# Three Sturm rounds of 7 points instead of two of 20, and 22 pairs of samples beside the Householder steps instead of 21

## The reference

```python
def reference(x, adj, L0_gnn_W1, L0_gnn_W2, L0_gnn_W3, L1_gnn_W1, L1_gnn_b1, L1_gnn_W2, L1_gnn_b2):
    def _slconv(x, adj, S, W):
        support = jnp.einsum('bnf,fh->bnh', x, W)
        return jnp.einsum('nm,bmh->bnh', adj * S, support)
    # layer 0, with S = adj: widths 256 -> 512 -> 1024 -> 256
    h = jnp.maximum(_layernorm(x, axis=-1), 0.0)
    h = jax.nn.relu(_slconv(h, adj, adj, L0_gnn_W1))
    h = jax.nn.relu(_slconv(h, adj, adj, L0_gnn_W2))
    x = x + _slconv(h, adj, adj, L0_gnn_W3)
    # layer 1: widths 256 -> 128 -> 256
    h = jnp.maximum(_layernorm(x, axis=-1), 0.0)
    deg = jnp.sum(adj, axis=0) + jnp.sum(adj, axis=1) - jnp.diagonal(adj)
    d = jnp.where(deg > 0, jax.lax.rsqrt(deg), 0.0)
    _, U = jnp.linalg.eigh(d[:, None] * (jnp.diag(deg) - adj) * d[None, :])
    agg = jnp.einsum('mn,bnd->bmd', U.T, h)
    out = jax.nn.relu(agg @ L1_gnn_W1 + L1_gnn_b1) @ L1_gnn_W2 + L1_gnn_b2
    return x + jnp.einsum('nm,bmd->bnd', U, out)
```

## Time and profile before

| | us |
|---|---|
| median of three runs (lowest, highest) | 2318.28 (2315.64, 2318.72) |
| profiled execution, span | 2315.7 |
| TensorE matmul busy | 2285.6 (99%) |
| TensorE weight load busy | 1884.1 (81%) |
| VectorE busy | 2018.1 (87%) |
| ScalarE busy | 1098.8 (47%) |
| GpSimd busy | 1102.6 (48%) |

### The profile page before, as it was taken

The page is one execution under the profiler, slowest core; times in us unless marked ns, Lnnn a source line. Parts: engine busy times, 40 slices in busy tenths (PEclk is TensorE's granted clock), DMA queues, the critical chain, the costliest instruction groups (busy, mean ns, idle before and its releaser), DMA issues.

```text
span 2315.7 us, 43479 instructions
## 1 busy us (share of the span) xinstructions
PE 2285.6 (99%) x11050; PEld 1884.1 (81%) x11050; DVE 2018.1 (87%) x10266; ACT 1098.8 (47%) x2581; POOL 1102.6 (48%) x1780
## 2 busy tenths in 40 slices
PE   7999999999999999999999999999999999999999
PEld 5777888787787788887777788888888888899998
DVE  8999999999999888878888889799999998467776
ACT  5445555555555444445444444444444444245554
POOL 6345545544444555455544464445555445243332
PEclk9999999999999999999999999999999999999999
DMA  2000000000000000000000000000000001024443
GB/s 103 28 28 28 19 19 28 28 28 25 22 28 28 28 20 18 28 27 28 28 28 28 19 29 28 28 10 28 27 27 27 28 28 37 19 67 130 135 132 108
DMA packets 90018, 89.95 MB, mean 39 GB/s; under 512 B 5376, under 2 KB 89088, under 8 KB 89856
## 3 DMA queue, kind: packets, MB, share of 16 engines
q1 hardware_dynamic: 89856, 88.23, 12.0%
HBM read 54.66 MB, written 33.55 MB: 38 GB/s over the span
## 4 chain that ended last, share of the span: by engine, by line
PE 83%; DVE 12%; ACT 2%; issue 2%; POOL 0%; DMA 0%; SPq 0%; POOLq 0%; DVEq 0%
PE ps L1481 68%; PE ps L1660 10%; PE ps L1393 3%; DVE A L895 2%; DVE A L899 1%; PE ps L1670 1%; ACT squares L624 1%; DVE xrow_sb L904 1%; PE ps L1607 1%; DVE qn L929 1%; ACT root_s L626 1%; DVE prods L932 1%; DVE sc L913 1%; DVE sc L916 1%; DVE qcol L918 1%
## 5 line engine op out<-in xcount | busy, mean ns | idle before, releaser
L1481 PE MATMUL ps<-w,hid2T 128*128 128x256 f32 x2048 | 465.9, 379 | 0.0
L1481 PEld LDWEIGHTS ps<-w,hid2T 128*128 128x128 f32 x2048 | 379.9, 190 | 49.8
L471 POOL COPY Eb<-sc 128x1 f32<-128x1 f32 (+1 forms) x254 | 47.2, 186 | 529.6 <-DVE v L920 297.2
L1481 PE MATMUL ps<-agg2T,w 128*128 128x256 f32 x1024 | 239.0, 379 | 0.0
L1481 PE MATMUL ps<-hid2T,xin 128*128 128x256 f32 x1024 | 235.8, 379 | 0.0
L1481 PE MATMUL ps<-weightT,hid 128*128 128x256 f32 x1024 | 235.6, 379 | 0.0
L1481 PE MATMUL ps<-w,aggT 128*128 128x512 f32 x512 | 231.8, 592 | 0.0
L1481 PEld LDWEIGHTS ps<-weightT,hid 128*128 128x128 f32 x1024 | 190.1, 191 | 35.2 <-issue 13.1
L1092 DVE RECIPROCAL ps<-ahead 128x40 f32<-128x40 f32 (+1 forms) x768 | 218.0, 329 | 0.1
L1481 PEld LDWEIGHTS ps<-agg2T,w 128*128 128x128 f32 x1024 | 190.2, 190 | 25.3
L1481 PEld LDWEIGHTS ps<-hid2T,xin 128*128 128x128 f32 x1024 | 189.3, 190 | 24.6
(11 more groups left out here) (370 smaller groups left out, 5547.7 us busy)
## 6 DMA issues: line engine op xcount, KB each, us to landing
xl<-in_x_dram SPq DMA_DIRECT2D x64, 256.0 KB, 2.9
xr<-in_x_dram SPq DMA_DIRECT2D x64, 256.0 KB, 2.9
x_dram<-xr SPq DMA_DIRECT2D x64, 256.0 KB, 2.3
xin<-x_dram SPq DMA_DIRECT2D x64, 256.0 KB, 2.8
out_dram<-xin SPq DMA_DIRECT2D x64, 256.0 KB, 2.1
w<-in_L_gnn_W_dram SPq DMA_DIRECT2D x1, 2048.0 KB, 10.6
w<-in_L_gnn_W_dram SPq DMA_DIRECT2D x1, 1024.0 KB, 12.2
w<-in_L_gnn_W_dram SPq DMA_DIRECT2D x1, 512.0 KB, 5.9
```

The costliest lines, as they stand in the source:

```text
L471: pool.tensor_copy(Eb[:, bass.ds(k, 1)], sc[:, 4:5])
L1481: ins = pe.matmul(dst, a, b, start=start, stop=stop)
```

## The change

Each of the 256 eigenvalues is now narrowed by three rounds of 7 points in place of two of 20: the interval shrinks by 8 x 8 x 8 = 512 in place of 21 x 21 = 441. W falls from 40 to 14. Three buffers get a size that holds 16 elements, for the first count. In `GROUPS`, pair 11 has 12 steps in place of 13, pairs 16 to 19 have 12 in place of 14, pair 20 has 11 in place of 13, and pair 21 now has 11 steps. So `WITH_STEPS` is 22 and `FIRST_ROUND` 24: the pairs without steps before the transposes of the counts are 22 and 23, the joins stand beside pair 24, and pairs 25 to 29 run alone.

```diff
-KS = 20
-ROUNDS = 2
+KS = 7
+ROUNDS = 3
...
         points = sb("points", [P, NB, KS])
-        negs = sb("negs", [P, ROUNDS_OF * 2 * NB * KS])
-        meet = sb("meet", [P, 3, NB * KS])
-        cnt = sb("cnt", [P, NB * KS])
+        widest = max(C0, NB * KS)
+        negs = sb("negs", [P, ROUNDS_OF * 2 * widest])
+        meet = sb("meet", [P, 3, widest])
+        cnt = sb("cnt", [P, widest])
...
-        GROUPS += [(8, 10, 12, 0.54), (10, 11, 12, 0.54), (11, 12, 13, 0.54), (12, 16, 12, 0.54), (16, 20, 14, 0.54),
-                   (20, 21, 13, 0.54)]
+        GROUPS += [(8, 10, 12, 0.54), (10, 11, 12, 0.54), (11, 12, 12, 0.54), (12, 20, 12, 0.54), (20, 21, 11, 0.54),
+                   (21, 22, 11, 0.54)]
...
-                link(dve.tensor_tensor(below_j[:, :, :], cnt[:, :].rearrange("p (a c) -> p a c", a=NB),
+                link(dve.tensor_tensor(below_j[:, :, :], cnt[:, 0:NB * KS].rearrange("p (a c) -> p a c", a=NB),
```

## The result

The changed kernel takes 2336.5 us (median of four runs, 2335.9 to 2338.1) against 2317.9 for the kernel before: a ratio of 1.008, 95% interval 1.0068 to 1.0092, so 16 to 21 us more, and 18.6 by the medians. The profiled execution has a span of 2336.3 us against 2315.7, 20.6 us more; its own time, 2338.07, is the highest of the four.

The account below looks back on a forecast made before the run. TensorE's matmul list bounds the kernel, so effects are waits: norm 49.9 - 19 - 2.8 = 28.1 us later, TensorE 27.7 later, plus 1.5 for the clock, 29.2 more. Forecast 2347.5 us, range 2336 to 2360.

Parts of the forecast that it names:

- the author's own case: The main forecast for the whole kernel: 2347.5 us, with a range of its own of 2338 to 2357; chance 0.76.
- The steps: TensorE beside pairs 11 to 21: fewer waits and moved steps make its list 8.8 us shorter, within 6 to 11.
- The start of the chain: VectorE's chain behind the transposes of the counts starts 49.9 us later, its 13.35 us wait staying.
- The rounds: VectorE's three rounds take 282 us, within 276 to 290, against 301.1 for two, so 19 us come back.
- The place: One of 128 places in a VectorE round, two reciprocals and two multiply-adds: 0.556 us with 14 elements.
- Company before the norm: Three VectorE instructions just ahead of the norm lose 2.8 us as GpSimd stands too; bounds 0 and 5.
- The standing: TensorE pauses 36 us in pair 30 before P5; ScalarE's square root waits near 41 us for VectorE.
- The clock: TensorE runs slow behind its pause in pair 30, losing 1.5 us, with 0 and 4 as bounds.
- the first: Rival: places no cheaper than with 16 elements, or more VectorE company in three rounds: 2359.5 us, chance 0.10.
- the third and fourth: Rivals on VectorE's place: 0.46 us, giving 2309.5 us, chance 0.04; about 0.48 us, no telling change, chance 0.02.
- a place of 0.76 us: VectorE's place by the skill page's rule of one cycle per element: rounds some 120 us, result about 80 us worse.
- The second: Rival: the square root holds nobody, TensorE stands only at L1619, from 1950.7; 2341 us, chance 0.08.

Follow-up runs that it names:

- e6: The changed kernel with GpSimd's sums made on 2 of 256 columns, so its output is not the reference's: 2319.0 us, ratio 1.0001.
- e5: The changed kernel with the joins of the reflectors from fragment 5 of pair 24 on instead of fragment 10: 2332.9 us, ratio 1.0064.
- e9: The changed kernel with 24 narrow VectorE instructions, forecast at 4.6 us in all, put in front of the first round: 2338.4 us, ratio 1.0088.
- e10: The changed kernel again, unaltered, on the same chip as the run with the delayed chain: 2337.3 us, ratio 1.0082.
- e3: The changed kernel with ScalarE's square root moved behind the evictions of P2 instead of those of agg2: 2338.2 us, ratio 1.0086.
- e4: The changed kernel with the transposes of the counts at fragment 27 of pair 23 instead of behind it: 2325.1 us, ratio 1.0030.
- e1: The kernel before with only the changed rounds, three of 7 points, and the old table of steps beside 21 pairs: 2317.8 us, ratio 0.9998.

## Why the prediction was right, and what was off

The direction and the mechanism were right. The size was not: 29.2 us more were forecast, 18.6 measured by the medians and 20.6 by the spans. The time of 2336.5 lies half a microsecond inside the range of 2336 to 2360, and below the 2338 to 2357 of the author's own case. That it lies inside at all is luck.

- **The mechanism** held step by step: no matmul more or less, TensorE's gain beside the steps, the chain that starts later, the pause in front of the second half of `hid2T,xin` in pair 30, released by ScalarE's eviction of P1, and no second wait at `turn_z`.
- **The steps.** Forecast 8.8 us, measured 9.15; pair 11 62.3 (62.28), pairs 16 to 19 246.0 (245.66), pair 20 61.1 (61.13), pair 21 64.1 (64.17).
- **The start of the chain.** Forecast 49.9 us later, measured 49.5, with the wait of 13.36 us unchanged.
- **The rounds: the term that was mis-sized.** Forecast 282 us, within 276 to 290, so 19 back; measured 272.55, 28.6 back. The place was right: 0.556 us forecast, 0.56 in the rows. What failed is the base it was put on: the 96.6 us of the one count with 16 elements were carried over whole, as a price of the walk. e6 has this count without company at 88.0 us and a round at 85, so some 9 us of company had been put into each of three rounds, where 4 to 7 belong. How much belongs depends on how VectorE's bulk instructions fall among GpSimd's sums: e5, e9 and e10 have 268 to 271 us for the same instructions. The forecast's rate for them, about 1 ns per element, was taken only for the difference between 16 and 14 elements; the whole of the count's bulk instructions, with their meetings in it, should have been taken apart.
- **Company before the norm.** Forecast 2.8 us, measured 1.9: from the eigenvalues to the square root 148.3 us before, 146.4 after. The three instructions did fall to 0.69 us each, but `before_y<-Db,lam` (L1161), just behind the eigenvalues, now met a sum and took 1.65 us instead of 0.69. That standing engines shorten the chain holds only for this stretch: e3 shows the cost of the sums moved, not removed.
- **The standing.** Forecast 36 us, measured 26.0, and ScalarE's wait 31.5 instead of 41: the 9 us of the rounds, and 1.6 by which TensorE came later to P5 than its gain beside the steps, since the pair with the joins was slow.
- **The clock.** Forecast 1.5 us; from P5 to `turn_z` it was 2.0, with a granted clock of 0.50 in the rows. The forecast's size came from a row that does not show the clock: in the stretches of 2 us around the 5.11 us at 12.87 the granted clock reads 1.00, and what slowed that row stays open. (The page's slices, digits of 9, say 0.9 or more.) The Trainium skill ("TensorE: Matmul & The Clock Gate", Part 1) says that the engine falls to half its clock when idle and returns once it has been busy; the trace agrees, with 0.50 behind the pause and 1.00 from 1966 on. The row of the 2.76 us wait, by which nothing would have been lost, was no guide to a pause of 26 us.
- **The sum.** 49.5 - 28.6 - 1.9 = 19.0 us for the square root; TensorE follows 0.75 us behind its start instead of 1.17, hence 18.6, plus 2.0 for the clock: 20.6, the difference of the spans.
- **The rivals.** The dearer place of the first, and the cheaper ones of the third and fourth, are out by the place of 0.56; the other half of the first (three rounds have more company than two) is out by rounds of 272.55 us. Out as well is a place of 0.76 us, with which the time would have been some 80 us longer. The second (the square root holds nobody) is out, since TensorE stood at P5. And where the square root was made to hold nobody, in e3, the time was not lower.

## What to carry to other kernels

When two chains run side by side and meet, write down the slack at each meeting before moving work between them. Here the slack was 0.5 us: of a delay of 19.0 us all but 0.4 reached TensorE, and an edit gained its time or nothing according to which chain was late. Count a moved stage by the whole period it is moved by (58.67 us), and what is given back by the instructions' own times, with the meetings of VectorE and GpSimd as a separate term. Two chains that look independent may be coupled by such meetings: here VectorE's rounds ended where TensorE's list, by way of GpSimd's sums, let them, and a few us put in front of them cost little (e9). A wait of an engine that the profile calls idle (the 13.36 us at L1136) is the first thing to take away once that engine's chain ends last (e4).

## What the runs showed of the hardware

- A VectorE instruction with two operands in SBUF that meets one of GpSimd's takes up to about 1 us longer. `Zsq<-Z` (128x512) took 1.64 us in the earlier trace rows and 0.69 in the changed kernel, where GpSimd stood; L1208 took 1.57 and 0.69. The wait ends with GpSimd's instruction: L1099, alone 0.61 us, took 1.69 when it started 0.1 us after the start of a sum and 1.03 when it started 0.7 us after it. It hits narrow instructions too: behind these sums `below_j<-cnt,index` (128x14) took 1.25 us, where `cnt<-meet` of the same size took 0.17. The walk, a reciprocal with one operand in SBUF and a multiply-add with one in PSUM, kept 227 ns with and without GpSimd's sums.
- TensorE's clock can fall after a pause as short as 2.76 us, and does not always. In the profiled execution of the kernel before it stayed at 1.00 behind the wait of the joins in pair 23 and the pair took 81.2 us; in e1 the same wait was followed by these stretches, and the pair took 84.3 us:

```profile
1547.00:1549.00 2.00, 1.60 (x4) 1.33 (x5) 2.00 (x12) 0.35 (x2) 0.00 (x0) 0.50 0.32 66
1549.00:1551.00 2.00, 2.00 (x7) 1.55 (x6) 2.00 (x14) 0.00 (x0) 0.00 (x0) 0.50 0.57 197
1551.00:1553.00 2.00, 2.00 (x6) 1.64 (x5) 2.00 (x16) 0.60 (x1) 0.00 (x0) 0.50 0.00 0
```

  In the changed kernel this pair took 82.8 us in one profiled execution and 81.2 in the other (e10). So one such wait can make this pair's time differ by up to 3 us between executions. That this is all of their scatter was not tested.
